# Taps from memory as block matrices, and five buffers that share space group by group

## The reference, cut to what matters

```
g1 = group_norm(x)
t1 = einsum('nchw,he->ncew', g1, p1)                 # 32 rows -> 16 mixed rows e
t3 = conv 9x9 of t1, each channel by itself (p3)
t4 = conv 5x1 of t3, groups of 4 channels (p4)
t5 = einsum('ncew,ewf->ncf', t4, p5)                 # f = 3*128
t6 = conv 1x3 of t5 along f, each channel by itself (p6)
x  = x + einsum('ncf,nfp->ncp', t6, three shifted rows of g1) / sqrt(3*128)
g2 = group_norm(x)
y  = 1x1 conv of [g2, three upsampled Haar details of g2] (conv_w)
out = x + relu(batch_norm(y))
```

## Time and profile before

| | us |
|---|---|
| median of 3 runs (383.11 to 384.33) | 384.11 |
| the profiled execution, whole | 386.18 |
| its span, first to last instruction | 384.4 |

### The profile page before, as it was taken

How to read it: one execution, slowest core, us unless ns; L and a number is a source line. 1 busy time by engine, 2 the same in 40 slices (tenths; PEclk the granted TensorE clock), 3 DMA queues, 4 the chain that set the end, 5 groups by cost and what they waited for, 6 DMA issues and landing times.

```text
span 384.4 us, 5177 instructions
## 1 busy us (share of the span) xinstructions
PE 303.8 (79%) x1679; PEld 246.9 (64%) x1679; DVE 328.2 (85%) x521; ACT 244.1 (64%) x400; POOL 266.2 (69%) x293
## 2 busy tenths in 40 slices
PE   0698756999999999269899999999999999784000
PEld 0244422999999995256788888888888887662000
DVE  1799987899999866969769999999999999669793
ACT  2389995576666669925565555666666555531791
POOL 9834555899998783396588988888888888852000
PEclk9999985999999999779999999999999999696555
DMA  8999910000342328935000000000000000000299
GB/s 178 168 200 214 195 38 3 1 2 0 80 104 54 69 49 229 403 141 218 0 3 1 2 1 0 2 0 0 3 0 2 0 2 0 0 1 2 110 401 363
DMA packets 18623, 31.08 MB, mean 81 GB/s; under 512 B 4292, under 2 KB 12228, under 8 KB 18596
## 3 DMA queue, kind: packets, MB, share of 16 engines
q1 hardware_dynamic: 18404, 30.32, 28.7%
q0 software_dynamic: 192, 0.42, 0.4%
HBM read 17.89 MB, written 8.39 MB: 68 GB/s over the span
## 4 chain that ended last, share of the span: by engine, by line
POOL 30%; ACT 21%; DVE 18%; PE 15%; issue 10%; DMA 2%; SPq 2%; DVEq 0%; POOLq 0%; ACTq 0%
POOL g_lo L477 9%; POOL g_lo L450 8%; PE wide L767 6%; ACT y_sb L642 5%; DVE x_sb L1107 4%; ACT d_split L588 4%; ACT t_hi L501 3%; DVE s_lo L918 3%; POOL rs L462 3%; POOL rs L458 2%; POOL rs L461 2%; ACT t_f L507 2%; ACT toe L512 2%; DMA p_raw<-in_p 2%; DVE d_split L970 2%
## 5 line engine op out<-in xcount | busy, mean ns | idle before, releaser
L641 ACT ACTIVATE g_hi<-x_sb,rs 128x1024 fp32r<-128x1024 f32 x16 | 21.5, 1342 | 51.1 <-POOL rs L462 51.1
L418 POOL TENSOR_TENSOR s_f<-toe,ci_mask 128x640 f32<-128x640 f32 x32 | 40.7, 1272 | 13.5 <-DVE s_lo L920 13.5
L477 POOL TENSOR_TENSOR g_lo<-y_sb,g_hi 128x1024 fp32r<-128x1024 f32 x15 | 36.1, 2404 | 17.6 <-ACT y_sb L642 17.6
L231 PE MATMUL wide<-g_hi,t_hi 128*128 128x512 f32 x96 | 39.3, 409 | 0.5
L918 DVE TENSOR_TENSOR s_lo<-s_f,s_hi 128x640 fp32r<-128x640 f32 x32 | 35.4, 1105 | 4.7 <-ACT s_hi L527 4.6
L900 DVE STREAM_TRANSPOSE xa<-x_ring 128x1024 f32<-128x1024 f32 x16 | 32.2, 2023 | 8.2 <-DMA x_ring<-in_x 7.9
L233 PE MATMUL wide<-g_hi,t_lo 128*128 128x512 f32 x96 | 38.2, 398 | 0.0
L232 PE MATMUL wide<-g_lo,t_hi 128*128 128x512 f32 x96 | 38.2, 398 | 0.0
L450 POOL TENSOR_TENSOR g_lo<-y_sb,g_hi 128x1024 fp32r<-128x1024 f32 x15 | 36.0, 2401 | 0.9 <-ACT g_hi L611 0.9
L1043 DVE SCALAR_TENSOR_TENSOR y_sb<-zh,y_sb 128x512 f32<-128x512 f32 x32 | 33.8, 1097 | 0.1
L526 ACT CAST s_hi<-s_f 128x640 fp32r<-128x640 f32 x32 | 23.4, 730 | 11.5 <-POOL s_f L421 11.4
(11 more groups left out here) (176 smaller groups left out, 1004.4 us busy)
## 6 DMA issues: line engine op xcount, KB each, us to landing
x_ring<-in_x SPq DMA_DIRECT2D x32, 256.0 KB, 6.0
x_sb<-in_x SPq DMA_DIRECT2D x8, 1024.0 KB, 7.1
out<-x_sb SPq DMA_DIRECT2D x7, 1024.0 KB, 5.0
d_sb<-t_out SPq DMA_DIRECT2D x58, 68.0 KB, 2.1
out<-x_sb SPq DMA_DIRECT2D x2, 512.0 KB, 2.6
p_raw<-in_p SPq DMA_DIRECT2D x8, 96.0 KB, 9.9
d_sb<-t_out POOLq DMA_DIRECT2D x6, 68.0 KB, 3.4
w_raw<-in_conv_w SPq DMA_DIRECT2D x1, 256.0 KB, 7.4
```

What stands on the lines that cost most here:

```text
L231: nc.tensor.matmul(ps, w[0], m[0], start=start, stop=False)
L418: pool.tensor_tensor(s3_f[:, g % 2], toe3[:, g].unsqueeze(2).broadcast_to([128, SHIFTS, CI, E]), ci_mask[:, :].unsqueeze(1).unsqueeze(3).b ...
L477: pool.tensor_tensor(g2_lo[:, :], y_sb[:, n, :], g2_hi[:, :].bitcast(F32), ALU.subtract).then_inc(s["g2_lo"], 1)
```

## The change

The taps aren't built on the chip. An input `taps` of 32 x 128 x 768 fp32 values (393 KB a group, 12.6 MB in all) holds, for each group, the block matrix and the mixing matrix ready made; so do inputs for `p1_blk`, `p5` in its final order, and the transposed `conv_w`. SyncE loads the taps group by group into `s_f` (a ring of `WR` = 4), ScalarE and VectorE split a group in one instruction each of 768 elements (rings of `SR` = 3). The products `toe3`, `toe4`, the masks, and GpSimd's work in stage B are gone.

`t1` has hi and lo of a group side by side and needs fewer zero columns. As the convolution leaves groups behind, their space is taken by `p5_hi`, `p5_lo`, `p5_raw` and then x. `d_sb` holds one batch only, so every batch is split into `d_split` before the next one is shuffled: ScalarE does one quarter (`d_high`) at the end of iterations 11 to 14, 19 to 22 and 27 to 30, VectorE follows one iteration later (`d_low`); the last batch is split behind the loop. p5 is split in iterations 15 to 18. Four of the eight reloads of x are issued in the stage B, in SyncE's loop over the taps, which issues the shuffles too. All 16 transfers of the last batch are SyncE's. All 17 of `t1_lo` are GpSimd's, from `t1_f`; `ps_t1` has four banks in place of two. The first image comes as a transfer of its own, and the order of the four 32-partition pieces is 0, 2, 1, 3. The weights of the second block are formed in the first two steps of stage C.

```diff
+WR, SR = 4, 3
+WCOLS = TAPS * C + C
+LATE_STATS = (2, 1, 2, 1, 2, 1, 2, 1)
+AGGR_AT, ST1_AT, GST_AT = 8, 12, 15
+P5_RAW_CONV, P5_AT = 7, 15
+D_AT = (11, 19, 27)
+RELOAD_IN_B = 4
...
+        p5_groups = groups_below(end_raw)
+        x_groups = [groups_below(at_x + 4 * HW * 2 * (k + 1)) for k in range(N // 2)]
...
+        def load_taps(eng, g):
+            eng.dma_start(s_f[:, g % WR, :], taps_in[g]).then_inc(s_in[g % WR], 16)
...
+            load_x(sp, x_slot[0][:, 0:1, :], 0, 1, x_in_first)
+            sp.dma_start(p1_blk[:, :], p1_blk_in).then_inc(s["p1_in"], 16)
+            load_x(sp, x_slot[0][:, 1:2, :], 1, 2, x_in[0])
...
+            def shuffle_batch(b):
                 sp.wait_ge(s["t4_ev"], GB * (b + 1))
                 if b == 0:
                     sp.wait_ge(s["x_used"], 2 * N)
+                else:
+                    sp.wait_ge(s["d_lo"], b)
+                shuffle(sp, b)
+
+            for g in range(3, G):
+                if g >= WR:
+                    sp.wait_ge(s["s_lo"], g - WR + 1)
+                load_taps(sp, g)
+                if g == P5_RAW_CONV + WR + 1:
+                    sp.wait_ge(s["conv"], p5_groups)
+                    sp.dma_start(p5_raw[:, :, :], p5_in).then_inc(s["p5_raw"], 16)
+                for k in range(RELOAD_IN_B):
+                    if g == max(x_groups[k], P5_AT + JC + 2) + WR + k:
+                        sp.wait_ge(s["conv"], x_groups[k])
+                        sp.wait_ge(s["p5_lo"], JC)
+                        reload_x(sp, k)
+                for b in range(NB - 1):
+                    if g == GB * (b + 1) + 1 + WR:
+                        shuffle_batch(b)
+            shuffle_batch(NB - 1)
+            sp.wait_ge(s["d_lo"], NB)
+            sp.dma_start(w_raw[:, :, :], w_in).then_inc(s["w_raw"], 16)
...
+                act.wait_ge(s_in[g % WR], 16 * (g // WR + 1))
+                if g >= SR:
+                    act.wait_ge(s["t4_mm"], g - SR + 1)
+                act.copy(s_hi[:, g % SR, :], s_f[:, g % WR, :]).then_inc(s["s_hi"], 1)
...
+            def d_high(b, jc):
+                act.wait_ge(d_in[b], 16 * JL * CI)
+                if b == 0 and jc == 0:
+                    act.wait_ge(s["x_used"], 2 * N)
+                src, hi, _ = split_views(b, jc)
+                act.copy(hi, src).then_inc(s["d_hi"], 1)
...
                 if g >= 1:
                     t4_evacuate(g - 1)
+                if P5_AT <= g < P5_AT + JC:
+                    jc = g - P5_AT
+                    act.wait_ge(s["p5_raw"], 16)
+                    act.copy(p5_hi[:, jc, :], p5_raw[:, jc, :]).then_inc(s["p5_hi"], 1)
+                for b in range(NB - 1):
+                    if D_AT[b] <= g < D_AT[b] + JC:
+                        d_high(b, g - D_AT[b])
+
             t4_evacuate(G - 1)
+            for jc in range(JC):
+                d_high(NB - 1, jc)
...
+                if t == 1:
+                    pool.wait_ge(s["w_hi"], 1)
+                    pool.tensor_tensor(w_lo[:, :, :], w_f[:, :, :], w_hi[:, :, :].bitcast(F32),
+                                       ALU.subtract).then_inc(s["w_lo"], 1)
```

More of the change, by code:

```diff
@@ L107, in build @@
+        d_split = put("d_split", [NO, 2, JC, C], F32R)
+        end_d = cursor[0]
+        cursor[0] = end_t
+        y_sb = put("y_sb", [N, HW])
+        assert cursor[0] <= end_d
+        cursor[0] = end_t
+        x_slot = [put("x_slot2", [2, HW])]
         xa = put("xa", [2, W, G])
-        p4_raw = put("p4_raw", [CI, 32])
-        p4_rows = put("p4_rows", [C])
+        t1_f = [put(f"t1_f{b}", [J, G]) for b in range(2)]
+        ones_row = put("ones_row", [HALF])
         p1_blk = put("p1_blk", [CI * E])
-        mask8 = put("mask8", [8])
@@ L112, in build @@
[L112 to L130, removed]
+        assert cursor[0] <= end_d
+        cursor[0] = end_d
+        s_f = put("s_f", [WR, WCOLS])
+        at_s = cursor[0]
+        s_hi = put("s_hi", [SR, WCOLS], F32R)
+        s_lo = put("s_lo", [SR, WCOLS], F32R)
         at_t3 = cursor[0]
@@ L198, in build @@
         ps_o, ps_y = wide
[L200 to L203, removed]
+        names = ("const ones pads zeros w_raw p5_raw p6_in p1_in xa x_used t1_mm t1_hi t1_f t1_lo "
+                 "w_det w_f w_hi w_lo s_hi s_lo conv t3_hi t3_lo t4_mm t4_ev d_hi d_lo p5_hi p5_lo u_part "
                  "st1 gst_mm gst gst_q rs1 t5 u_act u t6_mm t6_hi t6_lo g1_f g1_hi g1_lo o_half o_mm x1 "
@@ L559, in t4_evacuate @@
+            for i in range(NO):
+                t1_high(i)
             def t4_evacuate(g):
@@ L722, in _ @@
[L722 to L743 removed]
+                if i >= 4:
+                    pe.wait_ge(s["t1_f"], i - 3)
@@ L745, in t4_product @@
+                for v in range(2):
+                    rhs = xa[:, (i - 1) % 2, v:W:2, :] if i >= 1 else ones_row[:, :]
+                    mm = pe.matmul(ps_t1[i % 4][64 * v:64 * v + 64, :], p1_blk[:, :], rhs, start=True, stop=True)
+                mm.then_inc(s["t1_mm"], 1)
+            pe.wait_ge(s["ones"], 1)
+            pe.wait_ge(s["p1_in"], 16)
+            for i in range(NO):
+                t1_product(i)
             def t4_product(g):
@@ L834, in z_product @@
                 pe.wait_ge(s["g2_hi"], n + 1)
-                if n >= 1:
+                if n == 0:
+                    pe.wait_ge(s["w_lo"], 1)
+                else:
                     pe.wait_ge(s["z_ev"], n)
```

612 lines of the change are left out of this document (214 added, 398 removed).

## The result

| | before | after |
|---|---|---|
| median of the runs compared, us | 384.22 (383.11 to 384.38, 4 runs) | 392.58 (391.32 to 395.26, 4 runs) |
| profiled execution, us | 386.18 | 391.32 |
| its span, us | 384.4 | 389.6 |
| mean granted clock of TensorE | 0.914 | 0.874 |

The ratio is 1.0233, with an interval of 1.0169 to 1.0297: slower by more than the noise. The forecast was 389.8 us, slower. Executions over 1.5% slower than the fastest of their kernel are left out of every median and ratio here; only e3 had such, three of its ten, and with them its median would be 384.85 us. Beware of one thing in what follows: the profiled execution of before (386.18) lies 2 us over its timed runs and that of after (391.32) at the low end of its own, so the spans differ by 5.2 us where the medians differ by 8.4.

The account below looks back on a forecast made before the run. No engine bounds the whole span: VectorE binds stage A, TensorE stage B, GpSimd stage C. Terms -9.6 (A), +18.9 (B), +1.7 (to t5), -6.1 (t5), +0.8 (C) sum to +5.7: 389.8 us, 8-in-10 range 379 to 396.

Parts of the forecast that it names:

- The stall: Stage B: ScalarE waits for shuffled d, 5.5 us lost per batch; group 13 at X + 14.9, X being group 8's convolution end.
- The clock behind the waits: Stage B: after each wait TensorE runs at clock 0.50 for 3.5 us; 0.9 us counted per batch.
- The queue falls behind by some 5 us: Stage B: four x reloads beside the taps delay the DMA queue, which catches up before the next batch lands; priced at nothing.
- just covered: Stage B: a second wait, for taps issued behind the 16 shuffles, hidden by the first; 2 to 3 us if uncovered.
- Stage A: Start to first convolution matmul: 65.6 us becomes 56.0, -9.6, with less work on VectorE and an earlier first image.
- From B's end to t5: Last batch, issued by SyncE alone, then copies and split: 16.0 us becomes 17.7, +1.7.
- t5: First t5 to first output product: 17.0 us becomes 10.9, -6.1, as all of d is ready and no split interrupts.
- the second no longer starts at the low clock: Within t5: the second t5 product follows without a pause at a raised clock, saving 1.3 us.
- C and D: Output product to end: +0.8 us, from work in the first steps of C; the fixed cycle afterwards unchanged.
- Rival 1: Stage B: batches don't stall, d being in place by iteration 11; 370.5 us, 12% chance.
- Rival 2: Stage A and after pauses: x at the higher rate, -2.5, and clock rising at once, -3.7; 383.6 to 386 us, 12%.
- Rival 3: Stage B: loads of taps become the supply limit and the convolution waits for them; 395 or 396 us, 10% chance.

Follow-up runs that it names:

- e3: Changed kernel with GpSimd issuing 8 of each batch's 16 transfers and SyncE the other 8: 383.61 us, 0.9972 of the kernel before.
- e5: Changed kernel with the 16 transfers of each of the first three batches carrying only a quarter of their bytes: 388.34 us, 1.0094 of the kernel before.
- e7: Changed kernel with only one of four x reloads left in the convolution, three moved after the last batch: 390.63 us, 1.0171 of the kernel before.
- e4: Changed kernel with transfers issued by both SyncE and GpSimd, and the split of d one iteration later: 376.84 us, 0.9784 of the kernel before.
- e6: e4 with only one of four x reloads left in the convolution, three moved after the last batch: 370.52 us, 0.9644 of the kernel before.
- e2: Changed kernel with d's split starting in iterations 13, 21, 28 instead of 11, 19, 27, p5's in 17 instead of 15: 398.24 us, 1.0314 of before.
- e10: Changed kernel with x's four pieces issued in order 0, 1, 2, 3 instead of 0, 2, 1, 3: 392.42 us, 1.0209 of the kernel before.
- e9: e6 with 22 instead of 13 dummy products on TensorE ahead of t5: 368.39 us, 0.9602 of the kernel before.
- e8: e6 with 28 instead of 13 dummy products on TensorE ahead of t5: 372.56 us, 0.9678 of the kernel before.
- e1: Changed kernel with each of the first three batches copied in 4 plain transfers instead of 16, without rearranging d: 392.09 us, 1.0159 of the kernel before.

## Why the prediction was right, and where by luck

**The stall: right in place and kind, 4 us too small.** ScalarE stands at the first `d_split` of each batch, TensorE starts group 13 at 89.07, 15.4 us after X = 73.7 (14.9 forecast), and `s_hi` waits for no taps. e5 and e3 show that the number of issues in one queue is what costs. The size: TensorE's waits were 5.94, 7.12 and 6.75 in place of 5.5 each, 3.3 of the missing 3.9 us. Two things make them longer. From the first issue to ScalarE's copy it is 12.6, 12.9 and 12.7 us, not the 9.8 + 2.1 = 11.9 of a batch from which the queue carried nothing else: 2.5 us in three batches. e5 bears out that part of this is bytes: lighter transfers made the 16 issues 0.5 to 1 us shorter. And the second and third batch did not relate to their waits "in the same way": `t4_evacuate` was done at 101.25 and 129.09, but SyncE's first issue is at 102.72 and 129.81. In its order a load of taps stands ahead of the batch, and that load waits for VectorE's `s_lo` (done at 102.26 and 129.36), which was behind by then: 1.5 and 0.7 us.

**The clock behind the waits: right.** 0.50 in 88.9 to 92.6, 3.7 us where the earlier trace rows had 3.5.

**"The queue falls behind by some 5 us and has caught up before the batch behind it lands; I take nothing": right, in number and reason, for this kernel.** The third batch's first transfers landed 4.5 us late and its last at its usual 2.3, and e7, without this traffic, waits 6.62 us in place of 6.75. But what made it nothing were the 11 us of issues on top of it: e3, e4 and e6 show that with quicker issues the same backlog costs some 3 us (4.4 in e4, 1.25 in e6). Of the wait that was "just covered", that for the taps, the prediction gave a price, 2 to 3 us; e2 uncovered it at 4.8 us (3.7 at TensorE).

**Stage A: 3.6 us quicker than forecast.** x's first image is at 4.83 (5.4 forecast), image 2 at 12.4 (13.0), at 244 GB/s, and image 10 is reached at 36.84 (38.0). The last six images took 2.0 us each and not 2.15, and the last products 1.08 us: I had used the 1.98 us of a product at the low clock. That held until about 38 us (granted clock 0.50 in 20 to 38, products of 1.97), but for the last images the clock was up (1.00 in 44 to 50). With the shorter product the transposes alone set the pace. Behind the last product 0.6 more came in: `t1_hi` and `t1_f` took 1.6 us in place of 2.1. In all 1.2 + 0.9 + 0.9 + 0.6. The Trainium skill's "SBUF — State Buffer", section "Can I just issue two DMAs to hit both halves?", which says that transfers to two halves serialize, agrees with e10 (0.2 us and 5% of the rate by the order).

**From B's end to t5: right** (18.0 against 17.7; ScalarE's wait is 11.77).

**t5: 1.1 us too good.** The step that failed is "the second no longer starts at the low clock", -1.3. The first t5 took 3.98 us as forecast (4.0), but I had taken 3.5 us at the low clock, and here 18 matmuls took 0.52 or more, to 178.5, 6 us: six of them are the second t5's. The other -1.3, `u_mean`, came as forecast: 0.62 us in place of 1.90. e9 shows the whole price of that clock: 2.2 us.

**C and D: forecast +0.8, measured -1.4.** GpSimd's `g_lo` (208.10) came 6.96 us later than in the earlier trace rows where the output product was 6.56 later: +0.4. The rest was given back near the end, in the last steps of C, at a higher clock, as the stretches say, first of before, then of after:

```profile
326.30:343.70 17.40, 13.96 (x55) 11.28 (x55) 13.79 (x23) 6.68 (x14) 12.69 (x17) 0.80 0.00 0
```

```profile
333.00:348.90 15.90, 12.73 (x56) 10.20 (x55) 13.79 (x23) 6.64 (x13) 12.61 (x17) 0.89 0.00 0
```

The instructions are the same (but for one at the edge of the window), 1.5 us shorter at clock 0.89 against 0.80. On the side of the changed kernel it is not a chance of one execution: from the first output product to the end e6, e8 and e9 took 205.3, 204.9 and 204.5 us (after 205.0). Of before there is only the one profile, 206.3. Why the clock differs stays open; no run was made for it.

So errors of +3.9 (B), +0.3 and +1.1 (t5) met errors of -3.6 (A) and -2.2 (C). That the sum came within 0.5 us of the spans is luck; that the time gets longer, and by the stall, is not. Against the medians (+8.4) the forecast of +5.7 was 2.8 us low.

**The rivals.** Rival 1 (no stall, 370.5) did not happen. e6 comes to its number (370.52), but is no test of it: it still stalls 5.7 us at TensorE and shares the last batch too. Rival 2's quicker front came in size (-3.6) but not by its cause, for x came at 244 and not 411 GB/s; its milder clock did not come. Rival 3, the taps as supply, is out for the changed kernel: 0.0 us of waiting for them. Where `s_hi` does wait for taps (e2, 1.4 and 0.5 us in e4), the load stood behind the batch in SyncE's order or behind x in full DMA engines (share 1.04 in 113 to 126 us). The estimate from the "DMA: Bandwidth & Descriptors" page of the Trainium skill (2.7 us for one load) took one load at a time; here a load took 3.7 us to land, several were under way, and nothing waited for them.

## What to carry to other kernels

A batch of small transfers costs the issuing queue's time first: 16 issues were 10 us here whether they carried 68 or 17 KB, and everything else in that queue, and every in-order engine that waits for them, stands behind. Share the issues with a queue that is idle, place the consumer later only as far as the buffer's next use allows, and after each wait that goes look for the one that it covered: here issues, then taps, then the backlog of x, then the clock. Together these made 392.6 into 368.4 us, 4% under the kernel before.

## What the runs showed of the hardware

- 16 transfers from one partition block to another, 68 KB each, took SyncE 10.25 to 11.4 us, 0.60 us an issue in the median; with 17 KB, 10.1 to 10.9 us and 0.59. GpSimd issued the same in 0.55 us. The Trainium skill's "DMA: Bandwidth & Descriptors", section "Issuing engines are not separate DMA queues", says that issuing from several engines saves only the sequencer's time and that this is usually small beside the transfer. The first half agrees with e3, where SyncE's share of a batch is 5.4 to 6.4 us; the second does not hold here, where that time was 10 of 12 us.
- Four transfers of 272 KB over 32 partitions took 8.5 us each to land (median, e1), where sixteen of 68 KB took 2.1 to 2.5 each: fewer and larger was not faster.
- The same sum over 384 elements on VectorE (`u_mean`) took 0.62 us by itself and 1.88 and 3.77 us beside GpSimd's splits in the kernel before.
- In the same stretch of the same instructions the DMA engines, full in both, moved 322 GB/s in e4 and 261 in e6, on different chips, and the first wait for d was 0.2 us at TensorE in the one and 2.9 in the other:

```profile
75.00:87.00 12.00, 11.79 (x95) 11.68 (x95) 7.87 (x28) 8.75 (x18) 4.59 (x8) 1.00 1.05 322
```

```profile
75.00:87.00 12.00, 10.75 (x87) 10.64 (x85) 7.00 (x25) 5.98 (x13) 4.59 (x8) 1.00 1.03 261
```

e3, on e4's chip, has 297 GB/s there; e8 and e9 have 264 and 259 and first waits of 2.1 and 3.5 us. I had not expected that, and its cause stays open. It may be part of the 4 us over which the changed kernel's runs spread (391.3 to 395.3), but that is not shown: those of before spread over 1.3 us here and over 3.7 on another chip.
